# Graph network with layer norm on one core: degree chain behind the branch, layer norm's groups strewn through the index chain, first part's stores on the sync queue

## The reference

```python
def sage_conv(h, Wl, b, Wr):
    agg = segment_sum(h[src], dst, N) * inv_deg      # inv_deg = 1 / max(number of edges into a node, 1)
    return agg @ Wl.T + b + h @ Wr.T
h = maximum(layernorm(x), 0)
for layer in (0, 1, 2):
    h = leaky_relu(sage_conv(h, Wl[layer], b[layer], Wr[layer]), 0.01)
x = x + h
h = maximum(layernorm(x), 0)
g = h @ W                                            # attention, softmax over the edges into a node
e = leaky_relu((g @ att_src)[src] + (g @ att_dst)[dst], 0.2)
x = x + segment_sum(g[src] * softmax_by_dst(e), dst, N) + bias
```

## Time and profile before

| | us |
|---|---|
| median of 3 runs | 3276.03 |
| lowest and highest | 3267.15, 3280.86 |
| the profiled execution | 3295.59 |
| its span in the profile | 3293.9 |
| first part, to the first gather | 291.7 |
| DVE busy, share of the span | 60% |
| ACT busy | 43% |
| PE busy | 63% |
| POOL busy | 56% |
| PE clock granted, mean | 0.853 of full |

### The profile page before, as it was taken

One profiled execution on the slowest core, in us unless ns is written; L12 is line 12 of the kernel. 1 busy time (PEld: TensorE's weight loads), 2 busy tenths in 40 slices (PEclk: granted clock), 3 DMA queues, 4 the chain that ended last, 5 costly groups with the idle time before them and its releaser, 6 DMA issues. The chain is left out here.

```text
span 3293.9 us, 51342 instructions
## 1 busy us (share of the span) xinstructions
PE 2073.8 (63%) x12372; PEld 1809.0 (55%) x12372; DVE 1983.1 (60%) x8287; ACT 1403.5 (43%) x3736; POOL 1834.4 (56%) x1801
## 2 busy tenths in 40 slices
PE   0002677777784776767658989898864444555444
PEld 0001566666673665656547777777754444545444
DVE  7973444444452454544437888888856666666666
ACT  0494233333331222222214555555555555555555
POOL 1003666666646666666646666666635555555553
PEclk9999888899896888878879999999977777777777
DMA  3495566666664666666656777777754444555444
GB/s 98 149 324 170 164 187 197 186 191 189 194 191 114 202 194 192 194 195 199 187 166 188 223 214 219 222 219 220 221 159 118 120 126 123 130 130 126 124 123 111
DMA packets 600937, 576.11 MB, mean 175 GB/s; under 512 B 83405, under 2 KB 561311, under 8 KB 600608
## 3 DMA queue, kind: packets, MB, share of 16 engines
q1 hardware_dynamic: 395104, 311.69, 32.8%
q0 software_dynamic: 57360, 106.10, 14.8%
q10 hardware_dynamic: 148176, 155.01, 13.4%
HBM read 378.74 MB, written 207.75 MB: 178 GB/s over the span
## 5 line engine op out<-in xcount | busy, mean ns | idle before, releaser
L608 POOL DMA_INDIRECT rows<-tab,idx x1323 | 1364.4, 1031 | 880.7 <-issue 355.3
L829 PE MATMUL bank<-mask,rows 128*128 128x128 f32 (+1 forms) x3528 | 707.5, 341 | 160.8 <-issue 129.2
L1233 DVE TENSOR_TENSOR sage<-bank,sage 128x256 f32<-128x256 f32 x588 | 248.4, 423 | 862.8 <-remote 530.2
L829 PEld LDWEIGHTS bank<-mask,rows 128*128 128x128 f32 x3528 | 605.6, 215 | 227.7 <-issue 183.3
L608 POOL DMA_INDIRECT rows<-tab_c,idx x441 | 447.3, 1014 | 430.4 <-PE bank L939 175.8
L701 ACT ACTIVATE sage<-bank,b_col 128x256 f32<-128x256 f32 x392 | 184.9, 472 | 797.2 <-remote 433.5
L1213 DVE TENSOR_SCALAR mask<-iota,dcol 128x256 f32<-128x256 f32 (+1 forms) x1323 | 408.7, 342 | 0.0
L929 PE MATMUL bank<-ident,mask 128*128 128x128 f32 x784 | 171.2, 358 | 376.4 <-ACT mask L761 269.9
L929 PEld LDWEIGHTS bank<-ident,mask 128*128 128x128 f32 x784 | 124.2, 186 | 390.8 <-ACT mask L761 278.1
L781 ACT ACTIVATE sage<-cut_w,ed 128x256 f32<-128x256 bf16 (+1 forms) x441 | 184.7, 472 | 302.4 <-DVE ed L1424 287.4
L854 PE MATMUL bank<-sage,wcat 128*128 128x256 f32 x784 | 268.9, 429 | 50.8 <-issue 45.8
(11 more groups left out here) (212 smaller groups left out, 3476.5 us busy)
## 6 DMA issues: line engine op xcount, KB each, us to landing
sage<-inv_d SPq DMA_DIRECT2D x588, 128.0 KB
turned<-sage ACTq DMA_DIRECT2D x392, 128.0 KB
tab<-sage ACTq DMA_DIRECT2D x392, 128.0 KB
sage<-turned SPq DMA_DIRECT2D x392, 128.0 KB
tab_c<-sage ACTq DMA_DIRECT2D x196, 132.0 KB
own_w<-tab_c SPq DMA_DIRECT2D x196, 132.0 KB
tab<-sage ACTq DMA_DIRECT2D x49, 512.0 KB, 4.4
xin<-tab SPq DMA_DIRECT2D x196, 128.0 KB
```

The source lines that it names most:

```text
L608: eng.indirect_dma_start(out=rows[:, s.win[w], 0:width], out_offset=None, in_=table, in_offset=bass.IndirectOffsetOnAxis(ap=idx[:, s.w + w ...
L829: m = eng.matmul(to[:, a:b], rows[:, s.win[w], 0:D], mask[:, s.mw[w], c:c + b - a], start=(w == 1), stop=(w == 2))
L1233: eng.tensor_tensor(agg_t[:, o.r, :], ps[:, 0:TILE], own_t[:, o.v, :], ALU.add).then_inc(S["sum_v"], 1)
```

## The change

1. On DVE, the degree chain moves from the first part to the start of the fast path. Its store to `inv_d` moves from POOL to SP, which waits for the chain and for the store's landing in step 0 of phase 1, behind six loads of own features and before the first loads of inverse degrees. The waits for `inv_st` before phase 1 go.
2. The bias block moves from the start of the fast path to behind phase 2, and PE waits for it before phase 3.
3. `groups` is called in more places: 0 before the row search, then 1-2, 3-4, 5-7, 8-9, 10-11 inside the chain, one group behind each of the first seven moves of the closing of gaps (12 to 18), 19-24 before the windows, 25-28 behind them, 29-48 at the end.
4. SP issues the stores of the table. For each g it waits for the scaling of group g, stores it, waits for the landing of store g-1 and loads group g+6. Groups 1 to 4 are loaded before the weights, group 5 behind them.
5. The short last group of x is taken as eighth (`group_at`).
6. ACT copies the weights when it has four groups scaled, not first.

```diff
+def group_at(g):
+
+    return g if g < GR else NSG - 1 if g == GR else g - 1
...
             def load_g(g):
-                n = GTAIL // GJ if g == NSG - 1 else P
-                at = g * SG * TILE
+                n = GTAIL // GJ if group_at(g) == NSG - 1 else P
+                at = group_at(g) * SG * TILE
...
-            load_g(1)
+            for g in range(1, GAHEAD):
+                load_g(g)
...
-            for g in range(2, GAHEAD):
-                load_g(g)
-            for g in range(GAHEAD, NSG):
-                wait(eng, S[f"hg{g % GR}"], 16 * (g // GR))
-                load_g(g)
+            load_g(GAHEAD)
+            for g in range(NSG):
+                eng.wait_ge(S["h_a"], g + 1)
+                at = group_at(g) * SG * TILE
+                eng.dma_start(tab[0][at:at + SG * TILE, :].rearrange("(p j) d -> p (j d)", j=GJ), x_g[:, g % GR, :]
+                              ).then_inc(S[f"hg{g % GR}"], 16)
+                n = g + GAHEAD + 1
+                if n < NSG:
+                    wait(eng, S[f"hg{n % GR}"], 16 * (n // GR))
+                    load_g(n)
...
-            eng.wait_ge(S["inv_st"], 16)
...
+                    if ph == 1 and s.t == 0:
+                        eng.wait_ge(S["deg_v"], 1)
+                        eng.dma_start(inv_d[:, :].rearrange("(u q) e -> u (q e)", q=2),
+                                      deg[:, :, :].rearrange("u q e -> u (q e)")).then_inc(S["inv_st"], 16)
+                        eng.wait_ge(S["inv_st"], 16)
...
             for g in range(NSG + 1):
+                if g == GAHEAD:
+                    weights()
...
-                if o >= 1:
-                    store_g(o - 1)
-            store_g(NSG - 1)
...
-            eng.wait_ge(S["b_v"], 1)
...
+            eng.wait_ge(S["b_v"], 1)
```

More of the change, by code:

```diff
@@ L618, in scalar_program, with weights @@
         def scalar_program(eng):
[L620 to L634, removed]
+            def weights():
+                for n in range(7):
+                    eng.wait_ge(S["wt_ps"], n + 1)
+                    to = wcat[:, n // 2, (n % 2) * D:(n % 2 + 1) * D] if n < 6 else w_t[:, :]
+                    eng.activation(to, bank[n][:, 0:P], ACT.Copy).then_inc(S["wt_cp"], 1)
+                eng.activation(wg[:, 0:D], w_raw[:, 6, :], ACT.Copy).then_inc(S["wt_cp"], 1)
+                eng.wait_ge(S["wt_ps"], 8)
+                eng.activation(wg[:, D:D + 2], bank[0][:, 0:2], ACT.Copy).then_inc(S["wg_cp"], 1)
             for g in range(NSG + 1):
+                if g == GAHEAD:
+                    weights()
                 if g < NSG:
@@ L1030, in groups @@
                         scale_g(g - 1)
-            groups(0, 2)
+            groups(0, 1)
             eng.wait_ge(S["row_ld"], 32)
@@ L1040, in vector_program @@
             eng.sem_inc(S["prep_v"], 1)
+            groups(1, 3)
             eng.wait_ge(S["src_ld"], 16)
@@ L1050, in vector_program @@
             op(eng.tensor_reduce(stat[0:NAT_P, 2:3], cmp_m[:, :], AX.X, ALU.add))
+            groups(3, 5)
             eng.wait_ge(S["run_ld"], 64)
@@ L1088, in vector_program, with close_up @@
             eng.sem_inc(S["flag_v"], 1)
+            groups(10, 12)
             op(eng.tensor_copy(fill5[:, :], lead[:, :]))
             op(eng.tensor_tensor(fill5[:, 0:4], lead[:, 0:4], half_n[:, :], ALU.add))
-            def close_up(w, moves):
-                for b in range(moves):
-                    k = 1 << b
-                    op(eng.tensor_scalar(bit[:, :, 0:RUN - k], w[:, :, k:RUN], k, None, ALU.bitwise_and))
-                    op(eng.copy_predicated(w[:, :, 0:RUN - k], bit[:, :, 0:RUN - k], w[:, :, k:RUN]))
-            close_up(word, MOVES)
+            def close_up(w, b):
+                k = 1 << b
+                op(eng.tensor_scalar(bit[:, :, 0:RUN - k], w[:, :, k:RUN], k, None, ALU.bitwise_and))
+                op(eng.copy_predicated(w[:, :, 0:RUN - k], bit[:, :, 0:RUN - k], w[:, :, k:RUN]))
+            for b in range(MOVES):
+                close_up(word, b)
+                if b < MOVES - 1:
+                    groups(12 + b, 13 + b)
             eng.sem_inc(S["net_v"], 1)
@@ L1131, in vector_program @@
             eng.sem_inc(S["end_v"], 1)
-            groups(6, 8)
+            groups(25, 29)
             eng.wait_ge(S["ix_ps"], 1)
@@ L1140, in vector_program @@
                 eng.sem_inc(S["idx_g"], 1)
[L1143 to L1153 removed]
+            groups(29, NSG)
             scale_g(NSG - 1)
@@ L1266, in fast_vector @@
                 steps(eng, 5, phase)
+            for k in range(SP):
+                op(eng.tensor_scalar(is_part[:, k:k + 1], part[0:SP, 0:1], float(k), None, ALU.is_equal))
+            op(eng.tensor_copy(b_rest[:, 0, :], b_bc[0:SP, LAYERS - 1, :]))
+            for k in range(SP):
+                op(eng.tensor_copy(b_part[:, k, :], b_rest[:, k % 2, :]))
+                if k < SP - 1:
+                    op(eng.tensor_tensor(b_rest[:, (k + 1) % 2, :], b_rest[:, k % 2, :], b_part[:, k, :], ALU.subtract))
+            op(eng.tensor_scalar(b_sum[:, :], b_part[:, 0, :], is_part[:, 0:1], None, ALU.mult))
+            op(eng.scalar_tensor_tensor(b_sum[:, :], b_part[:, 1, :], is_part[:, 1:2], b_sum[:, :], ALU.mult, ALU.add))
+            op(eng.scalar_tensor_tensor(b_sum[:, :], b_part[:, 2, :], is_part[:, 2:3], b_sum[:, :], ALU.mult, ALU.add))
+            op(eng.tensor_copy(b_row[:, 0, :], b_sum[:, :]))
+            eng.tensor_copy(b_row[:, 1, :], b_sum[:, :]).then_inc(S["b_v"], 1)
             for r in range(RING):
```

45 lines of the change are left out of this document (16 added, 29 removed).

## The result

The changed kernel takes 3217.09 us, the median of four runs (3212.77 to 3222.67), against 3275.32 us for the kernel before: a ratio of 0.9828, 95% interval 0.9814 to 0.9843. That is 58.2 us less; the prediction said 59.5 less (3216.5). The profiled execution has a span of 3213.0 us against 3293.9, 80.9 less.

What follows compares the result with a forecast made beforehand. Bound: the first part, DVE and ACT waiting in turn until POOL's first gather at 291.7 us. First gather -64.5, start of phase 1 +5: -59.5, so 3216.5 us from a median of 3276.0; range 3199 to 3246.

Steps and rivals of the forecast that it cites:

- First gather 64.5 us earlier: End of the first part: POOL issues the first gather of phase 1 at 227.2 us instead of 291.7.
- ACT without gaps from 158: Last 20 groups of the first part: ACT scales from 158.3 at 3.27 us each, 65.4 us, to 223.7.
- The prediction's second account: First part, gain by causes: degree chain 30.3, weights 13, run_d wait 2.9, short group 5.7, 21 groups 13; 65 us.
- Stores on the sync queue, nothing: First part: 49 stores leave ACT's queue for SP; ACT gains no time and the loads stay hidden.
- the first rival: First part: one sync queue too narrow, last 20 to 30 groups follow store landings, 23 us lost, 3239.5; chance 0.11.
- The short group: First part: its 15 us load, issued about 38 and wanted about 56, is just covered; 0 to 5 us, not summed.
- Behind the branch, +5: Start of phase 1: the moved degree chain and late PE cost 5 us, bounds -5 to +16, slow gathers +7.
- one tile's gathers (2.9) and a little: Start of phase 1, reason for the +5 us: a late PE shifts POOL's first pause more than it adds one.
- rival 2: Phase 1 pays for the degree chain: PE's 16 us lateness plus 7 of slow gathers, +23, 3234.5; chance 0.12.
- gathers beside the degree chain take over 1.4 us: Start of phase 1: a sign named beforehand that would show the prediction wrong.
- First long pause at 32 to 42 us: Phase 1: POOL's first long pause comes 32 to 42 us after the first gather, three or four us earlier than before.
- Bias block, nothing: End of phase 2: the moved 3.7 us block fits where DVE idles 6.3 us for stores; cost nothing.

Runs made afterwards that it cites:

- 7: Changed kernel with the 49 table stores issued by ACT again, loads alone on the sync queue: 3249.6 us, 0.9833 of the kernel before.
- Experiment 10: Changed kernel with the short group of x loaded last again: 3217.2 us, 0.9841 of the kernel before.
- 3: Changed kernel with about 30 us of one-input tensor_scalar instructions in place of the degree chain: 2712.1 us, 0.9799 of the kernel before.
- 4: Changed kernel with the first nine masks ahead of the degree chain instead of behind it: 2717.1 us, 0.9819 of the kernel before.
- 6: Changed kernel without its degree chain, one memset to 1.0 in its place: 3243.5 us, 0.9810 of the kernel before.

## Right or wrong, step by step

- **The whole: 59.5 us less forecast, 58.2 measured.** It is 62.1 earlier less 3.9 given back, against 64.5 less 5. That the two agree to 1.3 us is more than the runs can tell: in the second set 50.9 us are gained and in the third 54.2 (stores on ACT), with first gathers 62 to 64 us earlier, so 3.9, about 12 and 9.7 us are given back by the times.
- **First gather 64.5 us earlier: 62.1.** Row search at 22.80 instead of 21.4, as row_d landed in 8.4 us (14.39 to 22.80) and not 7.0. From there to the last 20 groups 132.1 us, forecast 131.6. The scaling of the first of them at 161.00, not 158.3: ACT was two groups behind when the block began. Then 20 groups in 65.1 us (forecast 65.4) to 226.05, and 3.5 us to the first gather, as forecast. ACT without gaps from 158: right. The prediction's second account, the same sum from the other side, gives 65, but its parts miss one by one and cancel; the last point below has them.
- **Stores on the sync queue, nothing: right.** Shown by 7; the first rival (23 us) is out: not one wait for a load after 15 us.
- **The short group: covered, right.** It was issued at 41.32, and DVE took it at 56.19 without idling. What the prediction held open, a transfer queued behind it that waits, is there: the store issued at 44.98 had landed only when SP went on at 54.49, 9.5 us, against a median of 3.6, and it cost nothing. Experiment 10, which loads a full group in that place, shows that the short load is the cause: the two stores issued behind it land in 9.5 and 8.7 us in the changed kernel, and in 2.9 and 2.8 there. The Trainium skill's rule on the number of engines (DMA: Bandwidth & Descriptors, Why a DMA increments its semaphore by 16 and not by 1) gives a load of 106 partitions two engines; the slow landings behind it fit that.

```profile
41.32 0.25 SPq L409 DMA_DIRECT2D sage<-in_x  x1
44.98 0.33 SPq L441 DMA_DIRECT2D tab<-sage  x1
45.35 0.43 SPq L409 DMA_DIRECT2D sage<-in_x  x1
48.25 0.33 SPq L441 DMA_DIRECT2D tab<-sage  x1
54.49 0.33 SPq L409 DMA_DIRECT2D sage<-in_x  x1
```

- **Behind the branch, +5: the size fits, the reason was wrong.** The size is 5.3 to 6.1 us of phase 1 by the profiles of the third set; the times leave it open between some 4 and 12. The step that failed is "one tile's gathers (2.9) and a little", PE's lateness shifting the first pause. PE's lateness costs nothing that shows (experiments 3 and 4 without pauses, 6 and 7 with them). The cost is gathers beside the chain: 7.0 us over the first twelve, of which most is paid. The prediction had put them into rival 2 at +7, on top of 16 us of lateness, and beside two-input instructions only. It named "gathers beside the degree chain take over 1.4 us" as a sign that it is wrong, and the sign came: 2.24 us. That the time held all the same is luck: a cost that isn't there was put at nearly the size of one that the sum left out.
- **First long pause at 32 to 42 us: wrong, it comes at 56 to 62 us** (36 to 39 gathers instead of 34). The chain's end at 22, PE at 23 and the mean at 28 to 29 were right. POOL needs 51.6 us for 34 gathers instead of 44.2, the 7 us of the slow ones; why it is let on for two to five gathers more was not tried. Without the chain, in the third set, the first pause comes behind 34 gathers at 49.0 us as before. But in phases 2 and 3, beside which no chain stands, it comes behind 34, 36 or 39 as well.
- **Bias block, nothing: right.** DVE now waits 2.72 us for the stores behind it instead of 6.30, and the first gather of phase 3 comes 0.6 us behind this row as before.

```profile
1615.95 0.07 DVE L1287 MEMSET sage<- 128x16 f32 x1 [2.72 <-DMA tab<-sage]
```

- **What the parts are worth.** Spreading 22.5 us of first gather, the degree chain out of the first part 29.3, the short group's place 2.7, the stores 0 to 1: 54.5 of 62. The rest, 7.6, was not tried apart; most likely it lies in the weights behind the fourth group, with the row search at 22.8 instead of 34.4. The parts were taken away one at a time, so their sum need not be exact. Set beside the prediction's second account, the chain has 29.3 for 30.3, the run_d wait and the 21 groups 22.5 for 15.9, the short group 2.7 for 5.7 and the weights 7.6 for 13: it comes to 62 for 65 because too little for the spreading makes up for too much elsewhere.

## What to carry to other kernels

When two engines take turns at being the bound, count what the slower one of the last stretch (here ACT, 3.27 us for each group) stands idle before it: here interleaving the other engine's chain with its work bought just the idle time that it took away, 22.5 us for 22.2. Work moved behind the point that everybody waits for is cheap only if it leaves the engine alone that issues there: 30 us of DVE instructions cost 5 to 6 us of phase 1 where POOL has pauses and 9 in the time (with one more gather beside them) where it has none, through slower gathers and not through anyone waiting for their result. Compare profiles of one set, or set a profile's untouched phases side by side first: here 18 of the 81 us between two spans lay in phases that the change doesn't touch. And a gain of 2% of a kernel of 3.2 ms moved by 7 us from one set to the next: price a part by the event that it moves in the trace, not by the whole time.

## What the runs showed of the hardware

The same kernel before took 2768.7, 3270.9 and 3303.9 us in three sets, 19% between extremes, while the first part is as long in each (without the chain the first gather comes at 229.99 in the first and 230.47 in the third). What sets it can't be told from these runs. The instructions have the same durations (a gather 1.00 us, an addition of own features 0.42), the granted TensorE clock differs (0.93 against 0.85 to 0.86 as the mean of the span) and with it PE's busy time (474 to 478 against 504 to 509 us in phase 1), and so does the time from the end of PE's sum to DVE's addition that waits for it. The sixth sum of phase 1 and the addition that takes it, in the changed kernel:

```profile
264.97 1.11 PE L834 MATMUL bank<-mask,rows 128*128 128x256 f32 x6 [0.83 <-issue]
```

```profile
283.44 0.42 DVE L1235 TENSOR_TENSOR sage<-bank,sage 128x256 f32<-128x256 f32 x1 [10.13 <-remote]
```

and a later pair from the kernel without the chain in the first set:

```profile
272.53 1.11 PE L834 MATMUL bank<-mask,rows 128*128 128x256 f32 x6 [2.11 <-DMA rows<-tab,idx]
```

```profile
273.68 0.42 DVE L1226 TENSOR_TENSOR sage<-bank,sage 128x256 f32<-128x256 f32 x1 [2.98 <-PE bank L834]
```

From 264.97 + 1.11 to 283.44 is 17.4 us, and for the last 10.1 of them DVE stood idle, though the other two things that this addition waits for were done: ACT had copied the own features by 257.7, and PE had multiplied the tile four before by 263.9. 272.53 + 1.11 to 273.68 is 0.04. Over the 196 sums of phase 1 the median of this distance is 3.6 us in the changed kernel, 103 of them over 3 us; in the first set's kernel without the chain it is 0.04 us, and none is over 3. In all 196 cases of either kernel the own features were ready before the sum. The waits of DVE in phase 1 say it in one row each, the changed kernel first:

```profile
DVE sage L1235 <- remote: 245.0, 53, 6.8
DVE sage L1235 <- PE bank L834: 49.1, 33, 3.8
```

```profile
DVE sage L1226 <- PE bank L834: 249.0, 186, 5.5
```

So the 80 to 90 us of pauses in a phase, which the prediction took for the feedback of PE and POOL, go together with late news from PE: DVE stands idle in phase 1 of the changed kernel for 316 us in which all that it waits for is done, while PE's work is longer by 30 us. What makes the news late in one set and not in another stays open, and so does whether the lower clock is cause or consequence.
